# Graph network on one core: the five products with zeros ahead of a group's sum in attention are taken out

## What is computed

```
for l in range(2):
    q, k, v = projections of the normed nodes      # per node, 8 heads of 16
    att   = einsum('ehd,ehd->eh', q[dst], k[src]) / 4
    ex    = exp(clip(att))                          # per edge and head
    alpha = ex / segment_sum(ex, dst)
    aggr  = segment_sum(v[src] * alpha, dst)
    x = x + aggr @ Wo + bo
    x = x + gelu(layernorm(x) @ W1 + b1) @ W2 + b2
```

## Time and profile before

| | |
|---|---|
| median of 3 runs | 7133.87 us |
| the profiled execution | 7115.46 us, its span 7112.9 us |
| mean granted TensorE clock | 0.829 |
| PE busy (matmuls) | 4951.4 us, 70% |
| DVE busy | 3873.3 us, 54% |
| POOL busy | 3368.2 us, 47% |
| ACT busy | 678.4 us, 10% |
| PE L1758 (the products with zeros) | 370.6 us busy, 1228 records of matmuls |

### The profile page before, as it was taken

How to read it: one execution, slowest core, us unless ns; L and a number is a source line. 1 busy time by engine, 2 the same in 40 slices (tenths; PEclk the granted TensorE clock), 3 DMA queues, 4 the chain that set the end, 5 groups by cost and what they waited for, 6 DMA issues and landing times.

```text
span 7112.9 us, 114495 instructions
## 1 busy us (share of the span) xinstructions
PE 4951.4 (70%) x25317; PEld 3761.7 (53%) x25540; DVE 3873.3 (54%) x10619; ACT 678.4 (10%) x1598; POOL 3368.2 (47%) x3512
## 2 busy tenths in 40 slices
PE   2677656767778778887477666677777666666666
PEld 1121345555666656676455544566666444555555
DVE  8644346663344423444345556677667556666665
ACT  0011100000000000000001100011112100111111
POOL 0000265664555465553666566666443366665441
PEclk9975667668989989999688788899889788888887
DMA  1011323223333333343233244444333244443331
GB/s 47 18 54 72 116 74 91 83 81 104 116 116 120 105 115 112 110 128 104 61 116 98 77 120 120 123 121 121 104 100 87 80 121 118 123 120 104 92 90 49
DMA packets 308014, 695.45 MB, mean 98 GB/s; under 512 B 68843, under 2 KB 118116, under 8 KB 306526
## 3 DMA queue, kind: packets, MB, share of 16 engines
q0 software_dynamic: 146944, 381.90, 19.1%
q10 hardware_dynamic: 94612, 196.31, 8.2%
q1 hardware_dynamic: 66250, 114.82, 5.4%
HBM read 624.93 MB, written 67.83 MB: 97 GB/s over the span
## 4 chain that ended last, share of the span: by engine, by line
PE 32%; DVE 18%; issue 16%; DMA 14%; POOL 10%; DVEq 7%; ACT 2%; POOLq 0%; SPq 0%; ACTq 0%
DMA ring<-rows,idx_stage 12%; POOL ring L1391 10%; PE acc_ps L1853 7%; PE acc_ps L1835 7%; PE q_ps L1777 4%; PE acc_ps L1787 3%; PE bank L1889 2%; DVE wide L990 1%; DVE dots L993 1%; DVE even_rows L582 1%; DVE masks L808 1%; PE bank L2028 1%; PE acc_ps L1747 1%; DVEq L459 1%; DVEq L466 1%
## 5 line engine op out<-in xcount | busy, mean ns | idle before, releaser
L1391 POOL DMA_INDIRECT ring<-rows,idx_stage x3360 | 3329.0, 991 | 2482.3 <-DMA ring<-rows,idx_stage 914.5
L1853 PE MATMUL acc_ps<-ring,masks 128*128 x4800 | 1147.8, 400 | 681.9 <-SPq L1304 352.2
L1853 PEld LDWEIGHTS acc_ps<-ring,masks 128*128 128x128 f32 x4800 | 921.4, 241 | 879.7 <-issue 802.8
L1777 PE MATMUL q_ps<-odd_rows,conv_only 128*128 (+1 forms) x3904 | 733.5, 354 | 710.9 <-DVE conv_only L796 708.4
L788 DVE SCALAR_TENSOR_TENSOR masks<-dst_f,neg_first,lane 128x256 f32<-128x256 f32 x1200 | 546.1, 483 | 1057.7 <-PE acc_ps L1853 891.6
L1777 PEld LDWEIGHTS q_ps<-odd_rows,conv_only 128*128 128x128 f32 x3904 | 648.6, 255 | 782.0 <-issue 778.2
L1787 PE MATMUL acc_ps<-msg,masks 128*128 x3904 | 625.5, 309 | 191.2 <-DVE msg L1005 191.1
L1787 PEld LDWEIGHTS acc_ps<-msg,masks 128*128 128x128 f32 x3904 | 571.8, 216 | 318.3 <-issue 309.9
L1376 POOL COPY idx_stage<-src_idx 128x28 int32 (+1 forms) x126 | 33.1, 262 | 1157.0 <-DVE bias_part L727 809.5
L808 DVE SCALAR_TENSOR_TENSOR masks<-dst_f,neg_first,lane 128x512 f32<-128x512 f32 x488 | 366.6, 751 | 238.7 <-PE acc_ps L1787 231.0
L796 DVE TENSOR_SCALAR conv_only<-conv_only,node_id 128x512 f32 x488 | 243.6, 499 | 438.0 <-SPq L1333 267.3
(11 more groups left out here) (278 smaller groups left out, 6202.0 us busy)
## 6 DMA issues: line engine op xcount, KB each, us to landing
conv_only<-dst_rows SPq DMA_DIRECT2D x394, 256.0 KB, 3.3
ring<-rows,idx_stage POOLq DMA_INDIRECT x3360, 2.8
adjacency<-odd_rows ACTq DMA_DIRECT2D x10, 3136.0 KB, 8.8
conv_only<-adjacency ACTq DMA_DIRECT2D x70, 384.0 KB, 4.4
msg<-adjacency ACTq DMA_DIRECT2D x60, 384.0 KB
wide<-adjacency ACTq DMA_DIRECT2D x60, 384.0 KB, 4.4
turn_b<-adjacency ACTq DMA_DIRECT2D x60, 384.0 KB, 4.2
part<-adjacency ACTq DMA_DIRECT2D x30, 448.0 KB, 3.7
```

What stands on the lines that cost most here:

```text
L1391: pool.indirect_dma_start(ring[:, j, 0:WIDTH[p]], None, tables[p][:, :], bass.IndirectOffsetOnAxis(ap=idx_stage[:, half, j:j + 1], axis=0) ...
L1777: ins = pe.matmul(to, mask_t[:, u, j, :], q_rows[:, bass.ds(t + u, 1), :].rearrange("p a f -> p (a f)"), start=u == 0, stop=u == nxt)
L1853: ins = pe.matmul(to, masks[:, u, j, :], rhs, start=False, stop=final and j == GC - 1)
```

## The change

`wait_busily` is deleted, with its two calls. The wait for `q_used` in front of the products goes with them; all other waits stand as they were.

```diff
-            def wait_busily(p, g):
-
-                pe.wait_ge(q_used, group_at(p, sweeps, g) + 2)
-                keep_busy(q_ps[:, bass.ds(g & 1, 1), :].rearrange("p a f -> p (a f)"), EDGE_FILL)
-
             def attend_first(p, t, at):
 
                 first = at[0]
                 spread_q(p, t, first + 1, 0)
                 if not (isinstance(t, int) and t == 0):
-                    wait_busily(p, first)
                     add_group(p, t - 1, first, True, 0)
...
                     with pe.Fori(first + 2, last) as g:
                         spread_q(p, t, g, 0)
-                        wait_busily(p, g - 1)
                         add_group(p, t, g - 1, False, 0)
```

## The result

The changed kernel takes 7246.66 us (median of 4 runs, 7238.24 to 7247.98), the kernel before 7133.61 us beside it: 1.0157 times as long, 95% interval 1.014 to 1.0175, that is 113 us slower. The forecast was 7204 us, 70 us slower, in a range of 7095 to 7280 us. The profiled execution of the changed kernel took 7245.89 us, with a span of 7244.1 us and a mean granted clock of 0.767 (0.829 before). The page shows 24090 weight loads against 25540 before, which is the 1450 that were taken out.

The account below looks back on a forecast made before the run. Gathers bound many-group attention tiles; TensorE and VectorE handing work to each other bound late ones. 32 us gained and 101 us lost gave +69, taken as +70, on the 7133.87 us median: 7204 us, range 7095 to 7280 us.

Parts of the forecast that it names:

- The removed wait worth nothing: Ahead of the sums: the wait for q_used costs 0, since the message's wait that stays already contains its condition.
- The many-group stretches cost nothing at whatever clock: Attention's many-group tiles: clock falls to about 0.6 at the same length, hidden in a group time of 6.3 us.
- The third rival: Attention much slower: more of the chain turns or many-group stretches become paced by TensorE; 7254 to 7406 us, chance 0.12.
- The clock of the late stretches: Four late and mixed attention stretches: clock falls from 0.82 to 0.89 to 0.77, taken from a convolution stretch 64% busy.
- its loss less its gain: Four late and mixed attention stretches: about 101 us lost to the lower clock, less 32 us gained from products removed.
- the quarter taken off: Two mixed stretches: of 44 us clock loss, 11 us fall behind gathers that are late anyway.
- Not spread evenly: Late tiles: TensorE is on the chain where it waited for VectorE, so more of its chain work turns slow.
- a factor of 1.5 on the 93 us: Four late and mixed stretches: 93 us of TensorE's chain turn if spread evenly; raised to 140 us, 112 us lost.
- Nothing is added: Whole edit: only weight loads, products and waits go, nothing new is queued; no cost was booked for it.
- the +69 forecast: Whole kernel: 32 us gained and about 101 us lost sum to +69, taken as +70 us.
- The direct gain of 32 us: Four late and mixed stretches: products hold 46 us of the chain, of which 0.7 is gained; ends 0 and 46 us.
- Half of throttled time as penalty: TensorE's chain work at the lower clock: skill's rule doubles it, 140 us lost instead of 112, forecast some 25 us later.

Follow-up runs that it names:

- e1: Kernel before without the five products in each place, its wait for q_used kept: 7241.2 us, ratio 1.0153.
- b1: Kernel before plus eight more products ahead of each tile's last spread: 7335.28 us, ratio 0.9893 on the slower chip; again on a faster chip 7051.68 us, 0.9888.
- b2: As b1, plus six more products ahead of the spread in attend_first: 7361.54 us, ratio 0.9922 to the kernel before, on the slower chip.
- e4: Kernel before with products and wait gone only from the loop of attend_rest (194 of 290 places): 7124.98 us, ratio 0.9994.

## Why the prediction was right, point by point

- The removed wait worth nothing: right (e1, 7241 us against 7247 us).
- The many-group stretches cost nothing at whatever clock: right, 360 us before and after at 0.84 and 0.59. The clock there fell as far as was said ("0.6 or so"). The third rival is out, for those stretches did not get longer.
- The clock of the late stretches: 0.77 was taken for all four, and 0.74 to 0.80 given as the sign. In stretches of like work it was 0.76, 0.82, 0.74 and 0.74, in the order of the earlier trace rows:

```profile
4509.00:5042.00 533.00, 359.14 (x1903) 319.66 (x1904) 351.97 (x921) 76.90 (x199) 303.33 (x317) 0.76 0.39 115
5042.00:5573.00 531.00, 366.56 (x2061) 321.38 (x2060) 346.46 (x980) 102.53 (x254) 220.90 (x236) 0.82 0.31 92
6068.00:6545.00 477.00, 298.80 (x1598) 272.44 (x1599) 305.04 (x781) 56.03 (x135) 273.46 (x285) 0.74 0.39 114
6545.00:7232.00 687.00, 436.22 (x2309) 399.70 (x2307) 403.05 (x1144) 100.37 (x217) 252.50 (x269) 0.74 0.27 79
```

  The clock of the convolutions' stretches was a fair guess for the mean. But the size by stretch was not right. The forecast's own terms, its loss less its gain, come to about 20, 40, 3 and 7 us in that order; the stretches grew by 33, 31, 27 and 37 us. The first layer fits (60 forecast, 64 measured) and the second does not (10 and 64 us). In the second layer the clock fell lower than was taken, to 0.74, and the largest part of the gain had been booked there, 0.7 x 25 us in the last stretch. The mixed stretches lost about as much as the others, so the quarter taken off for gathers that are late anyway was not borne out. The miss thus sits almost wholly in the second layer, and the total looks better than its parts.
- "Not spread evenly", a factor of 1.5 on the 93 us: right in kind, and its cause more definite than was said. The turn to the lower level falls on the two sums right behind the hole that the products had filled, 88 us longer in the late stretches. Most of the last spreads were at the lower level already, behind a hole of their own.
- "Nothing is added": this is the step that failed. The edit moved register arithmetic from ahead of the message's wait to behind it, 0.1 to 0.2 us a sum: 15 us in the late stretches by the distances, 19 to 31 us by medians. The diff does not show it; the count of ALU_OP on L1787 (111, then 474) does. With it out of the account, the clock net of the direct gain is what the kernel with one short product is above the kernel before, 7213.99 - 7131.6 = 82 us (74 to 98 by its interval), against the +69 forecast. So of the miss of 43 us, 15 to 31 us are the arithmetic that was put at nothing, and the other 12 to 28 us are the size of the net term.
- The direct gain of 32 us was not measured by itself: no run had a clock held up by other means with the late products away. So the split of the 82 us into that gain and the clock's loss stays open.
- Half of throttled time as penalty, the rule of the Trainium skill that was weighed ("TensorE: Matmul & The Clock Gate", section "HAM oscillation — how this bites in real kernels"): a sum took 2.17 us at the lower level against 1.19, 1.8 times and not 2, as for the spreads of the earlier trace rows. That the forecast by it would have come nearer the result (some 25 us more) is chance, for the missing terms are others: the arithmetic, and the second layer.

## What to carry to other kernels

Read a product that keeps the engine busy by what stands right behind it, not by the mean clock: 96 places of 290 carried 92 of 113 us, and the 194 in the loop, most of them where gathers set the pace, carried nothing as long as the 96 stood. Put such products into the longest wait of the engine that is on the chain; here products ahead of the last spread were worth 1.1% more, of which a part may be an earlier start. When an instruction is taken out, look at what it computed for its neighbours: addresses of a later instruction can slide behind a wait, and the counts of the sequencer's instructions by line show it.

## What was not expected of the hardware

- Two chips ran the same kernel before at 7131 and 7426 us, 4% apart. On the slower one the profile of the kernel with eight products puts 646.3 us of the idle time ahead of ScalarE's exponential (L1502) down to "issue" (nothing that the profile shows), which the kernel before on the other chip doesn't show at all. That is mostly another label: the whole idle time ahead of the exponential is 1715.1 us there and 1681.5 us in the kernel before. What did grow is VectorE's wait for the exponential ahead of the message, 181.6 us against 70.9 us. The cause of the slower chip stays open. The ratio of b1 was the same on both (0.9893, 0.9888), that of the one short product was not (1.0042, 1.0121).
  Two rows of its waits (who waited for whom: us in total, times, longest us):

```profile
ACT msg L1502 <- issue: 646.3, 124, 15.7
DVE msg L1005 <- ACT msg L1502: 181.6, 76, 8.0
```

- From the start of one ALU_OP of TensorE's sequencer to that of the next lies about 0.1 us (4208.39 and 4208.48 us above), though each lasts 32 to 36 ns; two of them behind a wait moved the sum by 0.19 us (0.44 against 0.25 us after the message).
- A higher clock by itself is not speed: b2 had 0.838 in the mean and was no faster than b1 with 0.824, and e4 lost 0.04 of the mean clock (0.791 against 0.829) and no time.
